# Turning the hidden tile of the last feed-forward in rounded fp32, by quarters, and moving one stash store in the first layer

## The reference, cut to what matters

```python
def activation_quant(x):
    scale = 127.0 / jnp.clip(jnp.max(jnp.abs(x), axis=-1, keepdims=True), EPS, None)
    return jnp.clip(jnp.round(x * scale), -128.0, 127.0) / scale
def bitlinear(x, w, b):
    xq = activation_quant(x)
    wq = weight_quant(w)
    return jnp.einsum('bsd,fd->bsf', xq, wq) + b
h = bitlinear(x, w1, b1)                 # 512 -> 2048
h = jax.nn.gelu(h, approximate=False)
h = layernorm(h, gamma, beta)
return bitlinear(h, w2, b2)              # 2048 -> 512
```

## Time and profile before

| what | us |
|---|---|
| runs shown | 3716.21, 3713.45, 3708.44 |
| their median | 3713.45 |
| the profiled execution | 3708.7 |
| its span in the trace | 3707.1 |
| first layer, up to its last addition to x | 0 to 727 |
| last feed-forward, from the end of the attention before it | 3500 to 3707 |

### The profile page before, as it was taken

One profiled execution on the slowest core, in us unless ns is written; L12 is line 12 of the kernel. 1 busy time (PEld: TensorE's weight loads), 2 busy tenths in 40 slices (PEclk: granted clock), 3 DMA queues, 4 the chain that ended last, 5 costly groups with the idle time before them and its releaser, 6 DMA issues.

```text
span 3707.1 us, 40267 instructions
## 1 busy us (share of the span) xinstructions
PE 3437.8 (93%) x12305; PEld 1947.9 (53%) x12322; DVE 3013.5 (81%) x4951; ACT 1759.9 (47%) x2748; POOL 623.9 (17%) x596
## 2 busy tenths in 40 slices
PE   7888888799999999899999899999999999999887
PEld 4667676544444444444445788655455455455443
DVE  8899998797979798789889867688388388388797
ACT  6878787633333223334443311255155155155297
POOL 2324251243433220134331000000000000000000
PEclk9899988999999999999999999999999999999998
DMA  4324241524342322443444300221021022021000
GB/s 156 133 65 148 66 147 59 196 86 147 102 153 93 137 84 92 156 153 97 149 156 175 145 24 23 104 70 60 31 70 60 21 70 70 20 70 64 32 12 34
DMA packets 91260, 345.73 MB, mean 93 GB/s; under 512 B 11841, under 2 KB 20161, under 8 KB 77793
## 3 DMA queue, kind: packets, MB, share of 16 engines
q1 hardware_dynamic: 61552, 226.90, 17.4%
q0 software_dynamic: 29552, 116.94, 9.6%
HBM read 280.88 MB, written 62.91 MB: 93 GB/s over the span
## 4 chain that ended last, share of the span: by engine, by line
PE 48%; DVE 27%; issue 14%; ACT 6%; DMA 3%; DVEq 0%; POOL 0%; ACTq 0%; POOLq 0%; SPq 0%
PE ps L1213 30%; PE ps L1610 6%; PE ps L1600 3%; DVE room L1782 3%; PE ps L1441 2%; DVE room L1786 2%; DMA room<-bc_scratch 2%; DVE room L1790 2%; PE ps L1493 2%; PE ps L1282 2%; DVE room L1852 1%; DVE room L1795 1%; DVE room L1850 1%; ACT room L871 1%; DVE room L2320 1%
## 5 line engine op out<-in xcount | busy, mean ns | idle before, releaser
L1213 PE MATMUL ps<-lnT,room 128*128 128x512 f32 x2240 | 987.0, 596 | 23.1 <-DVE room L2007 16.0
L1213 PEld LDWEIGHTS ps<-lnT,room 128*128 128x128 f32 x2240 | 426.0, 191 | 567.9 <-issue 525.5
L1213 PE MATMUL ps<-room 128*128 128x512 f32 (+2 forms) x1807 | 666.8, 524 | 49.6 <-ACT room L1138 21.1
L680 POOL TENSOR_TENSOR idle<-idle 128x1 f32<-128x1 f32 x268 | 447.1, 1668 | 1263.4 <-ACT room L881 434.6
L1213 PEld LDWEIGHTS ps<-room 128*128 128x128 f32 (+1 forms) x1824 | 289.9, 163 | 404.5 <-issue 258.4
L1441 PE MATMUL ps<-room 128*128 128x512 f32 x864 | 379.7, 597 | 8.5 <-DVE room L1961 8.5
L792 ACT ACTIVATE room<-room,small 128x511 f32<-128x511 f32 x256 | 163.6, 710 | 380.6 <-DVE room L1786 380.5
L1852 DVE TENSOR_TENSOR_SCAN room<-room 128x2048 f32<-128x2048 f32 x64 | 283.2, 4425 | 19.0 <-ACT room L871 13.8
L1786 DVE TENSOR_TENSOR_SCAN room<-room 128x2048 f32<-128x2048 f32 x64 | 283.4, 4428 | 5.9 <-DVE room L1782 0.9
L1441 PEld LDWEIGHTS ps<-room 128*128 128x128 f32 x864 | 165.1, 192 | 215.2 <-issue 208.3
L1112 ACT ACTIVATE room<-ps,stat 128x512 f32<-128x512 f32 x256 | 199.0, 777 | 137.3 <-DVE stat L2268 137.3
(11 more groups left out here) (284 smaller groups left out, 5105.1 us busy)
## 6 DMA issues: line engine op xcount, KB each, us to landing
room<-in_ffn SPq DMA_DIRECT2D x16, 2048.0 KB, 10.9
room<-bc_scratch POOLq DMA_DIRECT2D x128, 256.0 KB, 3.6
room<-kv_stash SPq DMA_DIRECT2D x64, 512.0 KB, 3.4
kv_stash<-room POOLq DMA_DIRECT2D x96, 256.0 KB, 2.4
room<-stash POOLq DMA_DIRECT2D x24, 1024.0 KB, 5.2
room<-in_ffn SPq DMA_DIRECT2D x20, 1024.0 KB, 5.1
room<-in_ffn SPq DMA_DIRECT2D x24, 768.0 KB, 5.6
room<-in_ffn SPq DMA_DIRECT2D x12, 1536.0 KB, 7.3
```

Of the source, the lines that this page charges most:

```text
L680: nc.gpsimd.tensor_tensor(idle[:, :], idle[:, :], idle[:, :], ALU.add).then_inc(zeros_added, 1)
L1213: last = nc.tensor.matmul(out, lhsT, rhs, start=(i == 0), stop=(i == len(parts) - 1))
```

## The change

Two independent parts. In the last feed-forward `b_hq` and its pass are gone: TensorE turns the rounded fp32 tile `b_ga` itself, in four quarters of 4 blocks, alternating between PSUM banks 5 and 6, and ScalarE takes the rounding constant off while it copies each quarter out. `gelu(u+2)` overwrites the tile that is being turned, so in ScalarE's step it now stands behind `take_hqT(u)`. In the first layer, SP's entry that stores `m_z` moves from n = 8 to n = 9, behind the load of row 9 and the small store of the next batch's rows.

```diff
@@ SP, first layer
                         if n == 9 and not last:
                             store_bc(0, b + 1, tile("x", 0)[0])
-                        if n == 8:
+                        if n == 9:
                             place = stashed(2, b)
                             sp.wait_ge(Du_ready, b + 1)
                             sp.dma_start(place, m_z).then_inc(Du_stored, 16)
@@ ScalarE, last feed-forward
                 def take_hqT(u):
-                    act.wait_ge(b_htr, u + 1)
                     act.wait_ge(b_mm2, u)
-                    nc.scalar.activation(b_hqT, psb(5, 2), ACT.Copy).then_inc(b_hT_ready, 1)
+                    for q in range(4):
+                        act.wait_ge(b_htr, 4 * u + q + 1)
+                        nc.scalar.activation(b_hqT[:, q * 512:(q + 1) * 512], ps[:, 5 + q % 2, :], ACT.Identity, bias=unrnd
+                                             ).then_inc(b_hT_ready, 1)
...
                     nc.scalar.activation(b_ga[j % 2], b_ga[j % 2], ACT.Identity, scale=sc2[:, j % 2:j % 2 + 1], bias=rnd
-                                         ).then_inc(b_round, 1)
-                    act.wait_ge(b_round, u + 1)
-                    act.wait_ge(b_htr, u)
-                    nc.scalar.activation(b_hq, b_ga[j % 2], ACT.Identity, bias=unrnd).then_inc(b_hq_ready, 1)
+                                         ).then_inc(b_hq_ready, 1)
 
                 def step(u, j):
                     quantize(u, j)
-                    if u + 2 < B * NT:
-                        act.wait_ge(b_hq_ready, u + 1)
-                        gelu(u + 2)
                     if u + 3 < B * NT:
                         take_xqT(u + 3)
+                    take_hqT(u)
+                    if u + 2 < B * NT:
+                        gelu(u + 2)
                     if u + 2 < B * NT:
                         deviations(u + 2)
-                    take_hqT(u)
@@ TensorE, last feed-forward
                     pe.wait_ge(b_hq_ready, u + 1)
-                    for f in range(NF):
-                        mm = nc.tensor.transpose(psb(5, 2)[:, f * P:(f + 1) * P], b_hq[:, f * P:(f + 1) * P], identb_)
-                    mm.then_inc(b_htr, 1)
+                    for q in range(4):
+                        if 4 * u + q >= 2:
+                            pe.wait_ge(b_hT_ready, 4 * u + q - 1)
+                        for f in range(4):
+                            mm = nc.tensor.transpose(ps[:, 5 + q % 2, f * P:(f + 1) * P],
+                                                     b_ga[u % 2][:, (4 * q + f) * P:(4 * q + f + 1) * P], ident[:, :])
+                        mm.then_inc(b_htr, 1)
 
                 def out(u):
-                    pe.wait_ge(b_hT_ready, u + 1)
+                    pe.wait_ge(b_hT_ready, 4 * u + 4)
                     pe.wait_ge(b_done, u)
```

More of the change, by code:

```diff
@@ L267, in flamingo @@
         b_w = bit_w.bitcast(BF16)
-        (b_ga0, b_ga1, b_hq, b_hqT, b_tmp, b_dev) = split(h_out, F3, F3, F3 // 2, F3 // 2, D, F3 // 2)
+        (b_ga0, b_ga1, b_hqT, b_tmp, b_dev) = split(h_out, F3, F3, F3 // 2, D, F3 // 2)
         b_b1, b_gamma = h_P[:, 0:F3 // 2], h_PT
@@ L278, in flamingo @@
         b_w1, b_w2 = b_w[:, 0:NK * F3], b_w[:, NK * F3:]
-        b_xqT, b_hq, b_hqT, b_dev = (v.bitcast(BF16) for v in (b_xqT, b_hq, b_hqT, b_dev))
+        b_xqT, b_hqT, b_dev = (v.bitcast(BF16) for v in (b_xqT, b_hqT, b_dev))
         def psb(bank, n=1):
@@ L349, in flamingo @@
         b_mean, b_sq = sem("b_mean"), sem("b_sq")
-        b_scale_ready, b_round, b_hq_ready, b_htr, b_hT_ready, b_mm2, b_done = (
-            sem("b_scale_ready"), sem("b_round"), sem("b_hq_ready"), sem("b_htr"), sem("b_hT_ready"), sem("b_mm2"), sem("b_done"))
+        b_scale_ready, b_hq_ready, b_htr, b_hT_ready, b_mm2, b_done = (
+            sem("b_scale_ready"), sem("b_hq_ready"), sem("b_htr"), sem("b_hT_ready"), sem("b_mm2"), sem("b_done"))
         LNT = {1: 0, 2: 1, 3: 2, 5: 3, 6: 4}
```

## The result

| | us |
|---|---|
| before, 4 runs | 3712.81 median (3708.44 to 3716.21) |
| after, 4 runs | 3753.84 median (3748.07 to 3757.25) |
| ratio | 1.011 (95%: 1.0092 to 1.0127) |
| forecast | 3746 (3724 to 3770) |
| profiled execution after | 3753.04, span 3751.5, mean granted clock 0.963 |

The account below looks back on a forecast made before the run. The prediction took VectorE to bound the last feed-forward at 11.05 us per tile; loop 30.6 plus clock 14 minus first layer 11.8 gave 32.8 us more, forecast 3746 us, range 3724 to 3770.

Parts of the forecast that it names:

- The sign and the mechanism: Slower by more than 7.4 us, chance 0.90; last feed-forward: gelu waits for the turn's copies, closing a one-tile loop.
- The loop's length: Last feed-forward: 13.45 us per tile, every fourth 0.22 + 0.49 more, mean 13.6 against 11.05.
- the whole term: Last feed-forward: 12 turns of the loop at 2.55 us more each, 30.6 us; bounds 22 and 36.
- its two ends: Last feed-forward, before and after the loop: the old chain stays, copies replacing the old passes, counted at nothing.
- The clock: Last feed-forward: TensorE's idle lowers its clock in 10 of 12 tiles at 1.38 us each, 14 us.
- the bound of 28: Last feed-forward: upper bound of the clock's cost, all twelve tiles with turns and products at half speed, 12 x 2.3 us.
- The first layer: Moved store removes waits for row 9: 2.4 us arrive in three batches, 4.6 in the last, 11.8 saved; bounds 0 and 18.4.
- The clock stays up: Rival, last feed-forward: TensorE keeps its upper clock in nearly all tiles; 19 us slower, 3732 us; chance 0.17.
- The clock falls in every tile: Rival, last feed-forward: low clock in every tile, turns included; 47 us slower, 3760 us; chance 0.17.
- The loop does not bind: Rival, last feed-forward: VectorE keeps setting 11.05 us, only the moved store shows; 3702 us; chance 0.05.
- part 2 gives nothing: Rival, first layer: row 10 replaces row 9, or ScalarE's key/value wait stays; 45 us slower, 3758 us; chance 0.08.

Follow-up runs that it names:

- e4_third: Changed kernel with a third hidden tile and gelu(u+2) back behind quantize, ahead of take_hqT(u): 3695.09 us, 0.9962 of the kernel before.
- e6_pass_on: Changed kernel plus an extra 2.0 us ScalarE pass per step between take_hqT(u) and gelu(u+2): 3777.31 us, 1.0172 of the kernel before.
- e3_fill: Changed kernel plus ten unread TensorE products per tile between the turn and the hidden tile: 3726.77 us, 1.0046 of the kernel before.
- e10_buffer_only: Changed kernel with a third hidden tile, ScalarE's order left as changed: 3752.03 us, 1.0114 of the kernel before.
- e1_ffn_only: Changed kernel with SP's store back at n = 8, so only the last feed-forward's change: 3763.18 us, 1.0135 of the kernel before.
- e2_store_only: Kernel before with only SP's store moved from n = 8 to n = 9: 3702.52 us, 0.9972 of the kernel before.
- early order of keys and values: Kernel before with the store moved and one key/value tile moved from state 8 to state 7: 3699.1 us, 0.9966 of the kernel before.
- e5_pass_off: Changed kernel plus an extra 2 us ScalarE pass per step behind deviations(u+2), outside the loop: 3754.1 us, 1.0114 of the kernel before.

## Why the prediction was right, and where not

**The sign and the mechanism** held. The loop through turn, copies, gelu and products closed as described; e4_third opens it and the loss is gone, e6_pass_on lengthens it and the loss grows by that much. VectorE, first in the earlier trace rows, waits in every tile.

**The loop's length, 13.45 us and 0.71 more in every fourth tile,** came out at 13.49 and 0.69: e3_fill's periods of 13.71 and 13.96 stand 0.22 and 0.47 above 13.49, since the four extra blocks and the extra copy fall into neighbouring periods. The steps were right to 0.05 too: counted from 3562.89, the third quarter is turned 1.67 later (1.64 forecast), gelu starts 3.53 later (3.48), and the input of the next tile is turned 13.49 later (13.45). Nothing of this needed a row of the new operation itself; a copy with a bias column from another stage gave the right start-to-start time, 0.57.

That the whole term agrees too, 30.6 forecast and 31.3 measured (e3_fill against before), is in part luck: two steps failed and cancel. The loop closes with tile 0, not tile 1, so it is 13 periods and not 12: from the first turn to the fourteenth it is 142.2 us before and 177.3 in e3_fill, 35.1 more. And its two ends, counted "at nothing", gave back 3.8 us: 1.8 ahead of the first turn, where the removed pass stood on the chain, and 2.0 behind the fourteenth.

**The clock was the step that was mis-sized:** "10 of 12 times 1.38 = 14 us". It measured 22.5 for the stretch. The number of tiles was right, ten (of 13, though, and not of 12); the price was not. Of four consecutive periods three pay, and the four-tile pattern repeats: 16.31, 16.70, 14.96, 13.49, and again 16.30, 16.70, 14.95, 13.49. e10_buffer_only, which has the same periods and whose groups have all 36 records, shows that all of the extra lies in the products: they take 10.53, 10.67, 9.40 and 7.93 us, so 2.6, 2.7, 1.5 and 0 more than at full clock. Its ten slow groups of the loop add up to 22.2 us, 2.2 each. The price of 1.38 was taken from the earlier trace rows, where the clock was low for the first 3 us or so of a group of products; here it is low for the first 5.1 us (0.51 from 3582.40 to 3587.50), which at half speed costs 2.6. The turns were not stretched (1.04 and 1.24 us in both tiles above), so that part of the bound of 28 was empty. This term makes 8.5 us of error, about the 8 us of the sum by the medians (41 measured, 33 forecast). By the two spans the change is 44.4 us, and the rest of the 11.6 us of error is 0.7 from the loop with its ends and 2.4 from everything ahead of the last feed-forward (11.8 forecast, 9.4 in this pair of traces).

The Trainium skill's rule (TensorE: Matmul & The Clock Gate, "A second HAM failure mode: psum-queue depth-cycling") says that such a TensorE moves back and forth between its two clocks. The traces agree in that: the granted clock is 0.51 and then 1.00 within one group of products. They do not bear out what the prediction drew from it, that every tile would pay: three of four do in the changed kernel; in e6_pass_on all do.

**The first layer** was right in its mechanism: 11.8 us forecast; 9.3 by the medians with and without it (e1_ffn_only and the changed kernel), 6 to 15 by e2_store_only's interval; in the pair of traces 6.8 in the layer itself. Cut more narrowly, the traces say where the forecast held. In batches 0 to 2, from the softplus ahead of it (116.85 before, 116.90 after, in batch 0) to the one behind state 10 (168.63 and 165.58), they give 3.1, 2.7 and 1.9 us where 2.4 each was forecast, and from the last softplus to the end of the layer 3.5 where 4.6 was: 11.2 us in all. The missing 4.4 us were lost elsewhere in the layer, 3.7 of them in one stretch from softplus to softplus (399.8 to 459.3 before, 394.1 to 457.3 after) in which VectorE now waits 3.4 us for ScalarE's silu of the next batch (L807). No step of the prediction has such a wait, and it comes and goes from trace to trace (below). The wait for a row went, none came at state 10, and the wait for exp grew, from 2.18 to 3.85 in batch 0 (some 4.5 forecast), because GpSimd and ScalarE came 2.48 us earlier (157.59 to 155.11; 2.4 forecast). That the price of the marking addition depends on which instruction of VectorE it falls behind was the right reading of the earlier trace rows.

**The rivals.** The clock stays up (3732) fell with the 0.87 of the stretch. The clock falls in every tile (3760) was 6 us from the result, nearer than the forecast itself (8 us), but not what the trace shows: three of 13 groups keep their clock, and no turn is stretched. The loop does not bind, and part 2 gives nothing, fell by e3_fill and e2_store_only.

**Open.** What decides which tile of four keeps its clock; why the early order of keys and values did not shorten the wait for exp; and what makes the waits that scatter in the first layer (below). GpSimd's marker without its addition was not tried.

## What to carry to other kernels

Before an engine's pass is removed, ask who waits for that engine: a pass of ScalarE was worth 2 us in all beside VectorE's 11.05 us, and 23 us in the loop. When an in-place reader moves (a turn now reads the buffer that gelu overwrites), follow the overwriting instruction through each engine's fixed order until the path comes back to itself, and add that ring up; if it is longer than the present period, it is the new period, and one more buffer together with the old order opens it. And if a chain leaves TensorE idle on the critical path, don't price the clock by a single fall in the old trace (1.38 us here, against 2.2 in each tile that paid), or fill the gap with work that delays nobody.

## What the runs showed of the hardware that was not expected

- **The length of the idle does not decide whether the clock falls.** In e10_buffer_only two neighbouring groups of products stand behind the same 2.82 us of idle; one takes 7.93 us, the next 10.54. Behind 4.71 us (e6_pass_on) they take 9.65. The pattern isn't chance either: after, e1_ffn_only, e5_pass_off and e10_buffer_only all settle into the same four periods.
- **Idle filled with useless products is a gain:** 2.1 us of them per tile, 22.5 us less in the stretch.
- **Where the first layer scatters.** Its last addition starts, in seven traces whose first layer is the same program (the moved store), at 717.6, 720.5, 709.9, 709.6, 711.4, 723.1 and 718.3 us: 13.5 us apart. With the store unmoved: 724.3 and 728.0. The difference goes with VectorE's waits for ScalarE's silu of the next batch (L807), short in e3_fill (709.9), longer in the changed kernel (717.6) and longest in e6_pass_on (723.1):

```profile
DVE room L1816 <- ACT room L807: 2.2, 2, 1.2
```

```profile
DVE room L1812 <- ACT room L807: 6.2, 4, 2.2
```

```profile
DVE room L1814 <- ACT room L807: 13.1, 6, 3.8
```

  The four pieces around state 9 hold still: from softplus to softplus in batches 0 to 2, and from the last one to the end, they add up to 237.2 to 239.2 us in the seven traces, and to 248.8 and 246.0 in the two with the store unmoved. So a pair of traces cut at the layer's end prices part 2 at anything from 1 to 18 us, and a pair cut at these pieces at 7 to 12. What makes ScalarE's silu late isn't settled. The six stages between the first layer and the last feed-forward, the same program in all twelve traces, take 2766.3 to 2775.8 us.
- **GpSimd's addition of one column** took 3.96 us behind VectorE's scan and 1.73 us behind a product, at the same start (151.22 and 150.97): it came through when VectorE's instruction ended.
